# A vision layer on one core: the prologue of its attention part in another order, images 0 and 1 in buffers of their own

## The chip, the core and the metric

One core of a Trainium2 chip runs the whole program. The metric is the device time of one execution in microseconds (us); a kernel is given by the median of its runs. The engines are TensorE (PE, matmuls; PEld is its weight load), VectorE (DVE), ScalarE (ACT), GpSimd (POOL) and SyncE (SP, which here only starts transfers). They run side by side and wait for each other on semaphores that are written out by hand.

## What is computed

16 images of 5 x 128 x 128 are cut into 256 patches each of 320 numbers and embedded by a 320 x 256 matrix with a layernorm and `gamma`. Then comes one layer of 16-head attention whose scores are multiplied by a decay instead of a softmax, and one mixture of 8 experts:

```
h = layernorm(tokens @ W) * gamma
x = layernorm(h)
q, k = silu(x @ Wq), silu(x @ Wk);  v = x @ Wv
cum = cumsum(-softplus(x @ Wa + ba));  decay[i, j] = exp(cum[i] - cum[j]) for j <= i, else 0
o = groupnorm(((q @ k.T) * decay) @ v) * gn_w + gn_b
h = h + (o * sigmoid(x @ Wg)) @ Wo
h = h + top2_experts(layernorm(h))
```

## The kernel before

The attention part handles the images in eight pairs `p` of two images (512 columns), and each pair in eight steps `c` of two heads. `step(p, c)` exists once for every compute engine and lists, in a fixed order, what that engine does in this step: `scores`, `weighted`, `queries`, `keys`, `gates`, `values` on TensorE; `tanh_q`, `tanh_k`, `tanh_g`, `decay`, `keep_v`, `keep_o` on ScalarE; `silu_q`, `silu_k`, `decayed` on VectorE; `decay_rows` (the causal mask) on GpSimd. The same steps embed the images of the next pair, finish the attention of the pair before (groupnorm, `out_proj`) and route the rows of the pair before that. An engine never takes an instruction out of its order; a wait holds up all that stands behind it. The experts follow after the last pair and are not touched.

What matters here is the start, the steps of `p = -1`, in which only the work for pair 0 is done:

- An image's embedding: `load_patches(n)` (L351) brings 256 KB + 64 KB into `xt`; `tokens(n)` (L1105) makes 12 matmuls into bank 6; `embed(n)` (L1590) takes statistics and writes `h1`; `embed_rsqrt(n)` (L657) on GpSimd raises the variances to -1/2; `embed_norm(n)` (L1612) writes `xn1`; `turn(n)` (L1117) transposes it into bank 6; `keep_xnT(n)` (L747) copies that into `xs`; `scaled_h(n)` (L771) and `store_h(n)` send `h1` to DRAM. There is one `xt`, one bank, one `h1`, one `xn1` and one set of small statistics tiles for all images, so each image waits for the one before.
- The five weights `wv, wq, wk, wg, wo`, 1 MB each, come through three staging buffers in `big_f` (`load_weight`, L442). Each is split into a high part on ScalarE (`weight_hi`, L782) and a low part on VectorE (`weight_lo`, L1649), as every projection is made of three fp32r products. The pair's `xs` is split likewise (`xn_hi`, `xn_lo`).
- The decay: `logits(0)` (L1125), `decay_logits`, `softplus`, `log_decay`, `cum` (L1133), `running_sums`, `cum_rows`, `keep_cum` (L777); `store_cum(0)` writes the sums to DRAM and `load_decay` (L368) reads them back, spread over all partitions, in a ring of four; then `decay_rows`, `decay`, and `decayed`, which multiplies the scores.

All loads but some constants on GpSimd's queue are issued by SP, in this order: `wt`, patches 0, four constants, weight 0 (`wv`), patches 1, weights 1 and 2, `store_h(0)`, weight 3, patches 2, `store_h(1)`, weight 4, `store_cum(0)`, four decay loads. TensorE's own order of the start, by `step(-1, c)`: `tokens(0)`, `turn(0)`, `tokens(1)`, `turn(1)`, `logits`, `cum`, `cum_rows`, `tokens(2)`, `queries(0,0)`, `values(0,0)`, `keys(0,0)`, `values(0,1)`, `gates(0,0)`, and then `step(0, 0)` with `scores(0,0,0)`, `queries(0,1)`, `values(0,2)`, `values(0,3)`, `weighted(0,0,0)`. On ScalarE and VectorE the split of a weight stands at the head of a step:

```
            def start(c):
                if c == 0:
                    weight_hi(0)
...
            for c in range(NP):
                if c in (1, 3, 4, 6, 7):
                    weight_lo({1: 0, 3: 1, 4: 2, 6: 3, 7: 4}[c])
                step(-1, c)
```

Of the kernel before, what the change touches and what calls it, by code (L numbers as in the profile page):

```python
# [75 lines left out]
def vit_layer(nc, xT, w_tok, gamma, wq, wk, wv, wg, wa, ba, wo, gn_w, gn_b,  # L76
# [3 lines left out]
    with ExitStack() as ctx:  # L80
# [2141 lines left out]
```

## Time and profile before

| what | before |
|---|---|
| timed runs, us | 1323.49, 1326.96, 1327.07 |
| median, us | 1326.96 |
| the profiled execution: its time, us | 1323.79 |
| its span, us | 1321.9 |
| TensorE busy, us (share) | 1250.9 (95%) |
| ScalarE busy | 858.5 (65%) |
| VectorE busy | 825.2 (62%) |
| GpSimd busy | 428.1 (32%) |
| mean granted TensorE clock | 0.983 |

The span runs from the first to the last instruction. Busy time counts no waits. The granted clock is 1.00 at 2.4 GHz and 0.50 at 1.2 GHz. Matmuls are pipelined and their ends are modelled, so the busy time of TensorE says that it has work, not that it is at its peak. In the page's table of 40 slices (33 us each) the first slice shows TensorE 3 tenths busy, the second 8, every one of the others but the last 9 or more.

### The profile page before, as it was taken

The page shows a single profiled execution, that of the slowest core. Times are in us where ns is not written, and L with a number is a line of the kernel's source. Part 1 is how long each engine was busy: PE and PEld are TensorE (multiplying, and loading weights), DVE is VectorE, ACT ScalarE, POOL GpSimd, SP SyncE. Part 2 cuts the span into 40 slices and gives each one's busy share as a digit, 9 for nine tenths or more (in the row PEclk, how much of TensorE's full clock was granted, in tenths as well). Part 3 has the DMA queues.
Part 4 walks back from the last instruction along what each step waited for, and adds up shares of the span by engine and source line. Part 5 has one row for each costly group of instructions (what it writes and reads, how often), then busy time and mean ns, then how long its engine had stood idle before and what let it go on. Part 6 is the DMA issues. An engine that isn't in the chain of part 4 may idle for free. (4 is left out here: it accounts for less than half of the span.)

```text
span 1321.9 us, 27298 instructions
## 1 busy us (share of the span) xinstructions
PE 1250.9 (95%) x8534; PEld 1072.3 (81%) x8534; DVE 825.2 (62%) x2119; ACT 858.5 (65%) x2019; POOL 428.1 (32%) x524
## 2 busy tenths in 40 slices
PE   3899999999999999999999999999999999999996
PEld 2676777878778778778778778889999999989996
DVE  4455556665665665665665566657788888565552
ACT  2557577576576576576576565636788888666662
POOL 2021211241241241241141142164444544433434
PEclk7799999999999999999999999999999999999998
DMA  5321331341331331341332236458888787888873
GB/s 193 121 93 61 105 98 47 117 131 46 117 129 49 109 128 57 108 130 57 108 114 63 89 102 186 161 179 245 282 238 222 222 237 188 262 257 262 249 232 88
DMA packets 125607, 194.46 MB, mean 147 GB/s; under 512 B 16272, under 2 KB 91504, under 8 KB 125360
## 3 DMA queue, kind: packets, MB, share of 16 engines
q1 hardware_dynamic: 111920, 175.91, 41.5%
q0 software_dynamic: 13584, 17.26, 6.4%
q8 instruction: 54, 0.88, 0.3%
q14 instruction: 49, 0.40, 0.1%
HBM read 167.40 MB, written 29.05 MB: 149 GB/s over the span
## 5 line engine op out<-in xcount | busy, mean ns | idle before, releaser
L1161 PE MATMUL bank<-xn_sp,big_r 128*128 128x512 f32 x1152 | 312.1, 408 | 0.0
L1161 PEld LDWEIGHTS bank<-xn_sp,big_r 128*128 128x128 f32 x1152 | 204.6, 188 | 53.2 <-issue 1.4
L1674 DVE TENSOR_TENSOR att<-bank,dec_x 128x384 f32<-128x384 f32 x256 | 130.7, 552 | 110.1 <-PE bank L1198 108.9
L817 ACT ACTIVATE dec_x<-dec_x,ncum 128x256 f32<-128x256 f32 (+1 forms) x512 | 189.7, 444 | 5.7 <-POOL dec_x L654 5.7
L654 POOL TENSOR_SCALAR_AFFINE_SELECT dec_x<-dec_x 128x256 f32<-128x256 f32 x256 | 103.6, 434 | 215.8 <-DMA dec_x<-cum_scratch 215.7
L1494 PE MATMUL bank<-big_r 128*128 128x256 f32 x1296 | 168.0, 286 | 1.5 <-ACT mid_f L887 1.0
L1494 PEld LDWEIGHTS bank<-big_r 128*128 128x128 f32 x1296 | 160.5, 192 | 3.3 <-ACT mid_f L887 1.4
L705 POOL TENSOR_SCALAR mid_f<-mid_f,dec_x 128x256 f32<-128x256 f32 x71 | 76.9, 1087 | 187.0 <-DVE mid_f L1925 184.6
L711 POOL DMA_INDIRECT out<-mid_f,tok x71 | 118.6, 1671 | 53.0 <-POOL mid_f L705 22.0
L1941 DVE TENSOR_TENSOR big_r<-mid_f,big_r 128x256 fp32r<-128x256 f32 x216 | 91.4, 424 | 69.5 <-ACT big_r L907 69.3
L887 ACT ACTIVATE mid_f<-bank,h 128x256 f32<-128x256 f32 x216 | 101.2, 477 | 43.5 <-PE bank L1494 22.1
L789 ACT ACTIVATE tq<-bank 128x512 f32<-128x512 f32 x64 | 38.3, 598 | 140.3 <-PE bank L1161 140.3
L1932 DVE TENSOR_TENSOR big_r<-big_f,big_r 128x512 fp32r<-128x512 f32 x148 | 102.0, 695 | 7.1 <-ACT big_r L881 0.4
L1154 PE MATMUL bank<-big_r,xn_sp 128*128 128x512 f32 x384 | 97.7, 393 | 0.0
L1237 PEld LDWEIGHTS bank<-big_r,y_sp 128*128 128x128 f32 x768 | 95.5, 191 | 1.9
L1237 PE MATMUL bank<-big_r,y_sp 128*128 128x256 f32 x768 | 96.8, 284 | 0.0
L794 ACT ACTIVATE tq<-bank 128x512 f32<-128x512 f32 x64 | 38.2, 596 | 89.2 <-PE bank L1161 89.1
L1209 PE MATMUL bank<-att,mid_f 128*64 128x256 f32 x512 | 85.6, 407 | 10.4 <-ACT big_f L822 8.0
L1195 PE MATMUL bank<-q_s,k_s 64*128 64x256 f32 x512 | 91.0, 432 | 4.2 <-issue 4.2
L676 POOL DMA_INDIRECT expert_rows<-xn,slot x64 | 69.0, 1078 | 76.6 <-DVE slot L1809 60.4
L881 ACT ACTIVATE big_r<-big_f 128x512 fp32r<-128x512 f32 x148 | 93.5, 636 | 0.0
L907 ACT ACTIVATE big_r<-mid_f 128x256 fp32r<-128x256 f32 x216 | 91.7, 425 | 0.0
(217 smaller groups left out, 2231.4 us busy)
## 6 DMA issues: line engine op xcount, KB each, us to landing
big_f<-in_L_ffn_w SPq DMA_DIRECT2D x68, 1024.0 KB, 6.2
dec_x<-cum_scratch SPq DMA_DIRECT2D x128, 384.0 KB, 3.5
big_w<-in_L_ffn_w SPq DMA_DIRECT2D x12, 1024.0 KB, 6.7
mid_f<-expert_rows SPq DMA_DIRECT2D x27, 261.0 KB, 3.4
xt<-in_x SPq DMA_DIRECT2D x16, 256.0 KB, 3.7
h_scratch<-h SPq DMA_DIRECT2D x16, 256.0 KB, 2.3
h<-h_scratch SPq DMA_DIRECT2D x8, 512.0 KB, 4.3
out<-h SPq DMA_DIRECT2D x16, 256.0 KB, 4.0
```

The lines of the kernel that those rows point to most:

```text
L654: pool.affine_select(out=d, in_=d, pattern=[[0, 2], [1, P]], compare_op=ALU.is_ge, fill=fill, base=0, channel_multiplier=-1).then_inc(M["c ...
L711: pool.indirect_dma_start(out=out_rows, out_offset=bass.IndirectOffsetOnAxis(ap=tok[k.par][:, s:s + 1], axis=0), in_=yo[k.par][:, s, :], i ...
L817: act.activation(d, d, ACT.Exp, bias=ncum[p % 2][:, NS * u + s, 2 * c + hh:2 * c + hh + 1]).then_inc(M["exp_done"], 1)
L881: act.activation(parts[0].rearrange("p k n -> p (k n)")[:, cols], staged[:, cols], ACT.Copy).then_inc(M[f"{name}_hi"], 1)
L887: act.activation(target, bank[hbank[c % HB]][:, 0:width], ACT.Gelu_apprx_tanh, bias=b1_sb[k.par][:, c:c + 1]).then_inc(M["gel_done"], 1)
L907: act.activation(g_sp[0][:, c, :], gel[c % NGEL], ACT.Copy).then_inc(M["gh_done"], 1)
L1154: mm = pe.matmul(bank[target][:, :], xp[:, k, t * P:(t + 1) * P], wp[:, k, n * 512:(n + 1) * 512], start=(k == 0 and j == 0), stop=(k == E ...
L1161: mm = pe.matmul(bank[target][:, :], wp[:, k, c * P:(c + 1) * P], xp[:, k, :], start=(k == 0 and j == 0), stop=(k == EC - 1 and j == 2))
L1237: mm = pe.matmul(bank[target][:, s * E:(s + 1) * E], yp[:, j, u * S + s * P:u * S + (s + 1) * P], wp[:, GC * g + j, :], start=(j == 0 and ...
L1494: mm = pe.matmul(bank[hbank[c % HB]][:, 0:BLK], wp[:, i, c * P:(c + 1) * P], xp[:, i, :], start=(i == 0 and j == 0), stop=(i == EC - 1 and ...
L1674: dve.tensor_tensor(att[hh][:, :], bank[4 + hh][:, 0:LW], dec[n % RING][:, hh, :], ALU.mult).then_inc(M["mult_done"], 1)
L1932: dve.tensor_tensor(lo, staged[:, cols], f32(hi), ALU.subtract).then_inc(M[f"{name}_lo"], 1)
```

## The change

- Image 1 gets side buffers: patches, `h` and normed rows in parts of `mid_f` (where `v_sb` lies later), its small tiles in `pick`, which moves up; and bank 1. Image 2's tokens go to bank 7.
- Weights come in the order `wq, wv, wk, wg, wo`, with a staging buffer each for the first four; `wo` takes the second one again, after `ws_lo` 2.
- ScalarE issues the loads of `wt` and of the four constants, SP the rest in a new order.
- The loops over `step(-1, c)` give way to lists of functions on TensorE, ScalarE and VectorE. `values(0, 2)` and `values(0, 3)` and their copies are in the list, with banks 2 to 5 for the four, and no longer in `step(0, 0)`. The split of `wo` moves behind `step(0, 1)`.
- The waits follow: `tokens(0..2)` no longer wait for earlier images, `keep_v(0, 2)` and `keep_v(0, 3)` wait for image 1's side buffers, the first `scores` for the copies from banks 4 and 5.

```diff
-        stage_w = [big_f[:, i:i + 2048] for i in (0, 2048, 6144)]
+        stage_w = [big_f[:, i:i + 2048] for i in (0, 2048, 4096, 6144, 2048)]
...
+        side_x = [xt, mid_f[:, 2048:2048 + (KT + 1) * S].rearrange("p (k n) -> p k n", k=KT + 1)]
+        side_h = [h1, mid_f[:, 2816:3328].rearrange("p (s n) -> p s n", s=NS)]
+        side_n = [xn1, mid_f[:, 3328:3840].rearrange("p (s n) -> p s n", s=NS)]
+        little = pick[:, :, :, :].rearrange("p t k n -> p (t k n)")
+        side_st = [st1, little[:, 0:6].rearrange("p (s k) -> p s k", s=NS)]
+        side_su = [st1u, little[:, 6:12].rearrange("p (s k) -> p s k", s=NS)]
+        side_rs = [rs1, little[:, 12:16].rearrange("p (j s) -> p j s", j=2)]
+        side_ep = [eps0, little[:, 16:18]]
+        def of(n, buffers):
+            return buffers[1 if n == 1 else 0]
+        def embed_bank(n):
+            return {1: 1, 2: 7}.get(n, 6)
...
-        W_ATT = [wv, wq, wk, wg, wo]
-        w_parts = [wsp[2], wsp[0], wsp[1], wsp[3], wo_sp]
+        W_ATT = [wq, wv, wk, wg, wo]
+        W_IN = [("ws_in0", 1), ("ws_in1", 1), ("ws_in2", 1), ("ws_in3", 1), ("ws_in1", 2)]
+        w_parts = [wsp[0], wsp[2], wsp[1], wsp[3], wo_sp]
...
             def load_patches(n):
-                have(sp, "tok_ps", n)
-                image = xT[:, n * S:(n + 1) * S]
-                sp.dma_start(xt[:, 0:KT, :], image[0:KT * P, :].rearrange("(k p) n -> p k n", p=P)).then_inc(M["xt_in"], 16)
-                sp.dma_start(xt[0:KREM, KT, :], image[KT * P:FEAT, :]).then_inc(M["xt_in"], 16)
+                have(sp, "tok_ps", {1: 0, 2: 1}.get(n, n))
+                image, to, m = xT[:, n * S:(n + 1) * S], of(n, side_x), "xt_in1" if n == 1 else "xt_in"
+                sp.dma_start(to[:, 0:KT, :], image[0:KT * P, :].rearrange("(k p) n -> p k n", p=P)).then_inc(M[m], 16)
+                sp.dma_start(to[0:KREM, KT, :], image[KT * P:FEAT, :]).then_inc(M[m], 16)
...
+            def load_weight(i):
+                have(sp, "ws_lo", 2 if i == 4 else 0)
+                sp.dma_start(stage_w[i].rearrange("p (k n) -> p k n", k=EC if i < 4 else NP),
+                             W_ATT[i].rearrange("(k p) n -> p k n", p=P)).then_inc(M[W_IN[i][0]], 16)
             load_patches(0)
-            for dst, src in ((gammaB[:, :], gamma.rearrange("(a n) -> a n", a=1).broadcast_to([P, E])),
-                             (ident[:, :], ident_d),
-                             (baB[:, :], ba.rearrange("(a n) -> a n", a=1).broadcast_to([P, H])),
-                             (wa_sb[:, :, :], wa.rearrange("(k p) n -> p k n", p=P))):
-                sp.dma_start(dst, src).then_inc(M["c_in"], 16)
-            def load_weight(i):
-                have(sp, "ws_lo", i - 2)
-                sp.dma_start(stage_w[i % 3].rearrange("p (k n) -> p k n", k=EC if i < 4 else NP),
-                             W_ATT[i].rearrange("(k p) n -> p k n", p=P)).then_inc(M[f"ws_in{i % 3}"], 16)
+            load_patches(1)
             load_weight(0)
-            load_patches(1)
             load_weight(1)
+            load_patches(2)
             load_weight(2)
+            load_weight(3)
             store_h(0)
-            load_weight(3)
-            load_patches(2)
             store_h(1)
-            load_weight(4)
             store_cum(0)
             for c in range(2):
                 for u in range(2):
                     load_decay(0, c, u)
+            load_weight(4)
...
+            act.dma_start(wt[:, 0:KT, :], w_tok[0:KT * P, :].rearrange("(k p) n -> p k n", p=P)).then_inc(M["wt_in"], 16)
+            act.dma_start(wt[0:KREM, KT, :], w_tok[KT * P:FEAT, :]).then_inc(M["wt_in"], 16)
+            for dst, src in ((gammaB[:, :], gamma.rearrange("(a n) -> a n", a=1).broadcast_to([P, E])),
+                             (ident[:, :], ident_d),
+                             (baB[:, :], ba.rearrange("(a n) -> a n", a=1).broadcast_to([P, H])),
+                             (wa_sb[:, :, :], wa.rearrange("(k p) n -> p k n", p=P))):
+                act.dma_start(dst, src).then_inc(M["c_in"], 16)
...
+                if p == 0 and t >= NS and n == 0:
+                    act.wait_ge(M["tok_ps"], 2)
+                    act.wait_ge(M["h_out"], 32)
...
-            for c in range(NP):
-                start(c)
-                step(-1, c)
+            weight_hi(0)
+            weight_hi(1)
+            keep_xnT(0)
+            weight_hi(2)
+            keep_xnT(1)
+            xn_hi(0)
+            softplus(0)
+            scaled_h(0)
+            scaled_h(1)
+            tanh_q(0, 0)
+            keep_cum(0)
+            weight_hi(3)
+            for i in range(TP):
+                keep_v(0, i, 2 + i)
+            decay(0, 0, 0)
+            tanh_k(0, 0)
+            tanh_g(0, 0)
+            decay(0, 0, 1)
             for p in range(NPR):
                 for c in range(NP):
                     step(p, c)
+                    if p == 0 and c == 1:
+                        weight_hi(4)
 
...
+                if n == 1:
+                    pe.wait_ge(M["xt_in1"], 32)
+                else:
+                    pe.wait_ge(M["xt_in"], 32 * max(n, 1))
...
+                if n == 0:
+                    pe.wait_ge(M["v_done"], TP)
...
-                    if c == 0:
+                    if c == 0 and p > 0:
...
             tokens(0)
+            tokens(1)
             pe.wait_ge(M["c_in"], 64)
             pe.wait_ge(M["c_sum"], 32)
-            for c in range(NP):
-                step(-1, c)
+            turn(0)
+            tokens(2)
+            turn(1)
+            logits(0)
+            queries(0, 0)
+            values(0, 0, 2, "s1_xnT", 2)
+            values(0, 1, 3, "s1_xnT", 2)
+            cum(0)
+            values(0, 2, 4, "s1_xnT", 2)
+            cum_rows(0)
+            values(0, 3, 5, "s1_xnT", 2)
+            keys(0, 0)
+            gates(0, 0)
             pe.wait_ge(M["g_in"], 16 * 7)
...
-            for c in range(NP):
-                if c in (1, 3, 4, 6, 7):
-                    weight_lo({1: 0, 3: 1, 4: 2, 6: 3, 7: 4}[c])
-                step(-1, c)
+            embed(0)
+            embed_norm(0)
+            embed(1)
+            embed_norm(1)
+            weight_lo(0)
+            xn_lo(0)
+            decay_logits(0)
+            weight_lo(1)
+            log_decay(0)
+            weight_lo(2)
+            running_sums(0)
+            silu_q(0, 0)
+            weight_lo(3)
+            silu_k(0, 0)
             dve.wait_ge(M["g_in"], 16 * 7)
             dve.tensor_scalar(gnwh[:, :], gnw[:, :], 0.5, None, ALU.mult).then_inc(M["gnh"], 1)
             dve.tensor_scalar(gnbh[:, :], gnb[:, :], 0.5, None, ALU.mult).then_inc(M["gnh"], 1)
...
             for p in range(NPR):
                 for c in range(NP):
                     step(p, c)
+                    if p == 0 and c == 1:
+                        weight_lo(4)
```

In `embed`, `embed_norm`, `scaled_h`, `store_h`, `embed_rsqrt` and `turn` the tiles of image `n` are picked by `of(n, ...)`, and waits for the image before fall away for image 1.

## Rows read from the trace of the kernel before

**Rows 1.** Busy time by stretch: PE, PEld, DVE, ACT, POOL (x instructions), clock, DMA share, GB/s

```profile
6.30:40.00 33.70, 15.54 (x52) 12.53 (x52) 14.75 (x25) 13.37 (x15) 4.38 (x3) 0.65 0.58 192
57.00:350.00 293.00, 286.19 (x1825) 224.89 (x1824) 170.69 (x390) 186.08 (x415) 63.62 (x119) 1.00 0.28 91
```

**Rows 2.** Timeline of the prologue: start, us, engine, line, operation [idle before <- releaser]

```profile
1.84 0.56 SPq L354 DMA_DIRECT2D xt<-in_x  x1
...
6.33 4.46 PE L1113 MATMUL bank<-wt,xt 128*128 128x256 f32 x12 [6.33 <-DMA xt<-in_x]
...
10.90 0.70 DVE L1596 BATCH_NORM_STATS2 st<-bank 128x6 f32<-128x512 f32 x1 [9.39 <-PE bank L1113]
...
12.99 1.91 ACT L784 ACTIVATE big_r<-big_f 128x2048 fp32r<-128x2048 f32 x1 [11.00 <-DMA big_f<-in_L_attn_Wv]
...
13.67 1.05 POOL L660 TENSOR_TENSOR rs<-rs,mhalf 128x4 f32<-128x4 f32 x1 [7.03 <-DVE rs L1609]
...
14.93 2.29 DVE L1651 TENSOR_TENSOR big_r<-big_f,big_r 128x2048 fp32r<-128x2048 f32 x1 [1.35 <-ACT big_r L784]
...
18.02 1.08 PE L1122 MATMUL bank<-ident,turned 128*128 128x128 f32 x4 [7.24 <-DVE turned L1617]
...
19.88 4.51 PE L1113 MATMUL bank<-wt,xt 128*128 128x256 f32 x12 [0.78 <-ACT xs L753]
...
27.19 2.99 POOL L660 TENSOR_TENSOR rs<-rs,mhalf 128x4 f32<-128x4 f32 x1 [12.47 <-DVE rs L1609]
...
32.88 3.59 PE L1129 MATMUL bank<-wa_sb,xs 128*128 128x16 f32 x16 [0.69 <-ACT xs L753]
...
42.12 0.27 ACT L780 ACTIVATE cumT<-bank 64x128 f32<-64x128 f32 x1 [1.44 <-PE bank L1145]
```

**Rows 3.** Timeline from the cumulative sums to the first steps of the loop

```profile
42.54 5.12 PE L1113 MATMUL bank<-wt,xt 128*128 128x256 f32 x12 [0.45 <-ACT cumT L780]
...
50.93 1.48 ACT L817 ACTIVATE dec_x<-dec_x,ncum 128x256 f32<-128x256 f32 x4
...
52.32 0.58 ACT L794 ACTIVATE tq<-bank 128x512 f32<-128x512 f32 x1
...
52.93 0.69 DVE L1665 SCALAR_TENSOR_TENSOR k_s<-tq,bank 128x512 f32<-128x512 f32 x1 [2.54 <-ACT tq L794]
...
54.41 0.70 PE L1195 MATMUL bank<-q_s,k_s 64*128 64x256 f32 x4
...
56.76 2.90 PE L1154 MATMUL bank<-big_r,xn_sp 128*128 128x512 f32 x12
```

**Rows 4.** Busy time by stretch: the loads at the start

```profile
2.00:10.00 8.00, 3.67 (x10) 3.03 (x11) 0.00 (x0) 0.00 (x0) 4.64 (x9) 1.00 0.91 263
10.00:12.00 2.00, 0.78 (x4) 0.35 (x2) 1.07 (x2) 0.00 (x0) 0.00 (x0) 1.00 0.16 58
14.00:19.00 5.00, 0.98 (x4) 0.71 (x4) 2.94 (x3) 0.90 (x1) 0.72 (x1) 0.50 0.99 368
```

**Rows 5.** Timeline further on, at full clock: step (0,2), and the logits of pair 1

```profile
77.18 1.02 DVE L1674 TENSOR_TENSOR att<-bank,dec_x 128x384 f32<-128x384 f32 x2 [3.62 <-PE bank L1198]
...
78.49 2.75 PE L1113 MATMUL bank<-wt,xt 128*128 128x256 f32 x12
...
78.69 0.60 ACT L789 ACTIVATE tq<-bank 128x512 f32<-128x512 f32 x1 [1.74 <-PE bank L1161]
...
104.21 1.85 PE L1129 MATMUL bank<-wa_sb,xs 128*128 128x16 f32 x16
```

**Rows 6.** Busy time by stretch: where the granted clock changes

```profile
22.00:24.00 2.00, 2.00 (x7) 1.64 (x7) 0.00 (x0) 2.00 (x2) 0.00 (x0) 0.68 0.93 283
26.00:28.00 2.00, 0.00 (x0) 0.00 (x0) 1.93 (x6) 0.00 (x0) 0.81 (x1) 0.68 0.35 120
46.00:48.00 2.00, 2.00 (x8) 1.61 (x7) 0.00 (x0) 0.00 (x0) 0.00 (x0) 0.71 0.28 112
```

More of the change, by code:

```diff
@@ L946, in step @@
                     decay(p, c + 1, 0)
-                    for i, source in {0: ((2, 2), (3, 1)), 1: ((4, 2),), 3: ((7, 2),)}.get(c, ()):
+                    for i, source in {0: ((2, 2), (3, 1)) if p > 0 else (), 1: ((4, 2),), 3: ((7, 2),)}.get(c, ()):
                         keep_v(p, i, source)
@@ L980, in step @@
                     tanh_g(p, c + 1)
-            def start(c):
-                if c == 0:
-                    weight_hi(0)
-                if c == 2:
-                    weight_hi(1)
-                if c == 3:
-                    weight_hi(2)
-                if c == 5:
-                    weight_hi(3)
-                if c == 6:
-                    weight_hi(4)
-            for c in range(NP):
-                start(c)
-                step(-1, c)
+            weight_hi(0)
[16 more added lines that the diff above has]
+            decay(0, 0, 1)
             for p in range(NPR):
@@ L1112, in tokens @@
                     for k in range(KT + 1):
-                        mm = pe.matmul(bank[6][:, s * E:(s + 1) * E], xt[:, k, s * P:(s + 1) * P], wt[:, k, :],
+                        mm = pe.matmul(bank[embed_bank(n)][:, s * E:(s + 1) * E], of(n, side_x)[:, k, s * P:(s + 1) * P], wt[:, k, :],
                                        start=(s == 0 and k == 0), stop=(k == KT), skip_group_check=True)
@@ L1121, in turn @@
                     for s in range(NS):
-                        mm = pe.transpose(bank[6][:, k * S + s * P:k * S + (s + 1) * P], xn1[:, s, k * P:(k + 1) * P], ident[:, :])
+                        mm = pe.transpose(bank[1 if n == 1 else 6][:, k * S + s * P:k * S + (s + 1) * P], of(n, side_n)[:, s, k * P:(k + 1) * P], ident[:, :])
                 mm.then_inc(M["s1_tps"], 1)
@@ L1149, in values @@
                 t, n = i % TP, i // TP
+                if p == 0 and i == 0:
+                    pe.wait_ge(M["ws_lo"], 2)
                 pe.wait_ge(M["xl_done"], p + 1)
@@ L1593, in embed @@
                 dve.wait_ge(M["tok_ps"], n + 1)
-                have(dve, "h_out", 16 * n)
-                rows = bank[6][:, :].rearrange("p (s n) -> p s n", s=NS)
+                have(dve, "h_out", 16 * n if n > 1 else 0)
+                h1, st1, st1u, rs1, eps0 = (of(n, x) for x in (side_h, side_st, side_su, side_rs, side_ep))
+                rows = bank[embed_bank(n)][:, :].rearrange("p (s n) -> p s n", s=NS)
                 dve.bn_stats(st1[:, :, :].rearrange("p s k -> p (s k)"), rows.rearrange("p s n -> p n s")).then_inc(M["s1_st"], 1)
@@ L1600, in embed @@
                                              op0=ALU.subtract, op1=ALU.mult).then_inc(M["s1_u"], 1)
-                have(dve, "s1_h", NS * n)
+                have(dve, "s1_h", NS * n if n > 1 else 0)
                 dve.tensor_scalar(rs1[:, 0, :], st1[:, :, 2], 1.0 / E, EPS, ALU.mult, ALU.add).then_inc(M["s1_v0"], 1)
@@ L1613, in embed_norm @@
                 dve.wait_ge(M["s1_rs"], n + 1)
-                have(dve, "s1_tps", n)
+                have(dve, "s1_tps", n if n > 1 else 0)
                 have(dve, "lg_ps", 2 * (n // 2 - 2))
+                h1, xn1, st1u, rs1 = (of(n, x) for x in (side_h, side_n, side_su, side_rs))
                 for s in range(NS):
```

37 lines of the change are left out of this document (16 added, 21 removed).

## The prediction, made before the change was run

> **What bounds the kernel now.** I read the table of stretches first [rows 1]. From 57 to 350 us TensorE is busy for 286.2 of 293 us at a granted clock of 1.00; from 6.3 to 40 us it stands still more than it works (15.5 busy of 33.7 us). So the main loop is bound by TensorE, and what happens before the first `scores` is a serial prologue whose length goes straight into the time. The timeline of the prologue [rows 2] says what it waits for. Image 0: `tokens(0)` 6.33 to 10.79, its statistics, then 2.29 us of `weight_lo(0)` ahead of `embed_norm(0)`, so `turn(0)` starts only at 18.02. Image 1 can't start before image 0 has left `xt`, bank 6 and `h1`: `tokens(1)` at 19.88, and so on. Here GpSimd's power took 2.99 us beside a `weight_lo`, against 1.05 for image 0. Then `logits` at 32.88, `cum`, `cum_rows`, `keep_cum` at 42.12. From there a fixed chain leads to the loop [rows 3]: `keep_cum` at 42.12, the decay rows through DRAM (first exponential 50.93), `tanh_k` and `silu_k`. The first `scores`, at 54.41, comes right behind `gates`, so at that point the decay chain and TensorE end nearly together.
>
> The profiled execution took 1323.79 us for a span of 1321.9. Of the three timed runs one (1323.49) lies with it and two (1326.96, 1327.07) lie 3 us higher, the median among them. I sum against 1323.8 and correct at the end.
>
> **The change, part by part.**
>
> *Loads.* Six issues, some 0.56 us each, leave SP's queue for ScalarE's; two of them stood ahead of the patches of image 0 (issued at 1.84, rows 2), which now go out 1.1 us earlier. ScalarE pays the same issues in time in which it waits for the first weight (11.00 us idle before 12.99, rows 2), so they cost nothing; without that cover, 3 us. The 16 DMA engines are already 0.91 busy from 2 to 10 us [rows 4]. If bytes decide and three queues now share them, `tokens(0)` gains nothing or loses 0.5; if the issue decides it gains 1.1. I take 0.5: 5.8 to 10.3. The Trainium skill (DMA: Bandwidth & Descriptors, section "Issuing engines are not separate DMA queues") says that loads started on several engines run on the same 16 DMA engines and that only the issuing time is saved; by that the gain here would be near nothing, 6.3 instead of 5.8. Whichever bound `tokens(0)` takes, the end of the chain doesn't move, as the next part shows.
>
> *Bytes ahead of image 2.* In the new order SP issues patches 0, patches 1, Wq, Wv, and then, after `tokens(0)`, patches 2, Wk, Wg. TensorE's new order is `tokens(0)`, `tokens(1)`, `turn(0)`, `tokens(2)`, `turn(1)`: image 1's turn stands behind image 2's load. Up to the end of patches 2 that is 320+216 KB on ScalarE's queue, 292 KB on GpSimd's and 3 x 320 + 2 x 1024 on SP's: 3836 KB, 3.93 MB. By 10 us the old trace had moved 8 us x 263 GB/s = 2.10 MB; then SP's queue ran dry (58 GB/s to 12 us), which it no longer does. The other 1.83 MB at the 368 GB/s of Wq and Wk together (14 to 19 us) take 5.0 us, to 15.0; Wv's semaphore came some 2 us behind its bytes (the rate fell away at 10, it was used at 12.99), so patches 2 are there at about 16.8. Bound: 16.0 with one us of tail, 19.0 at the 263 GB/s of the first 10 us.
>
> *Images 0 and 1.* `tokens(1)` follows at once, 2.75 us at full clock [rows 5], 4.5 at half: 13.1 to 14.8. VectorE: `embed(0)` 10.4 to 13.2 (10.90 to 13.67, where GpSimd's power begins, before), power 1.05, norm 0.73: 15.0; `embed(1)` the same, 19.7. No `weight_lo` stands between. All of it is hidden under the load of patches 2. `tokens(2)` takes 4.5 at low clock, 16.8 to 21.3, `turn(1)` 0.7 to 22.1, `keep_xnT(1)` 0.6 to 22.7. ScalarE must have done `weight_hi(2)` by then: Wk lands 1.05/0.368 = 2.9 us behind patches 2, at 19.7, plus 1.91 [rows 2] is 21.6. Just in time; if it is late, `keep_xnT(1)` is queued behind it.
>
> *Logits to cumulative rows.* `logits` took 3.59 us at half clock [rows 2], 1.85 at full [rows 5]; I take 3.0: 25.9. `xn_hi`, `xn_lo` (1.04, 1.22) fit in, to 25.1. `zb`, `zm` to 26.4; `weight_lo(1)`, 2.28, to 28.7 with softplus (0.26 x 3 and a 1.28 table load) under it; `la` 28.9. `queries`, six matmuls like a `values`, is hidden under `weight_lo(1)`; `values` 0 and 1 wait for it. At 1.45 us each at full clock (two of them took 2.90, rows 3) and up to twice that at half, I take 4.1 for the two: 32.8. `cum` 0.8, 33.6; `running_sums` 0.5 while `values(2)` runs to 35.1; `cum_rows` 0.4, `keep_cum` 0.3: 35.85, against 42.39 before. The bounds are 34.5 (all at full clock) and 38.5 (all at half).
>
> *The fixed chain.* Store, decay loads and mask until the first exponential took 50.93 - 42.39 = 8.54 us. ScalarE now runs `weight_hi(3)` and four `keep_v` (1.9 + 4 x 0.6 = 4.3) under it and `decay(0,0,0)` ahead of `tanh_k`: 1.48 + 0.58 + 0.69 + gaps 0.1. Together 11.4: first `scores` at 47.3, 7.1 earlier. `weight_lo(3)` (37.8 to 40.0) and `gates` (to 41.6) are under it too, and TensorE idles from 41.6 to 47.3.
>
> *Work moved out of the loop.* `values` 2 and 3, 2.90 us on a TensorE that is busy without a gap [rows 1, 3], now lie in the prologue: gain 2.9. Their copies overwrite image 1's side buffers, so they wait for `h_out`: `scaled_h(1)` ends about 31, store 2.3 later, long before 37.8.
>
> *What is given back.* (a) Clock. The granted clock fell from 1.00 (2.4 GHz) to 0.50 (1.2 GHz) at 26.7, 2.3 us after `tokens(1)` had ended, and went up at 23.3, when TensorE had worked 3.4 us from 19.88, and at 47.2, 4.6 us from 42.54 [rows 2, 3, 6]; the moments are worked out from the mean clock of the 2 us stretches. After 5.7 idle us I count it low at 47.3: about 4 us of work at half speed, 2.0 lost. Bounds 0 and 2.3. (b) Wo's split. `weight_hi(4)` (1.91) and `weight_lo(4)` (2.29) move into the end of step (0,1). ScalarE waited 1.74 there and VectorE 3.62 [rows 5]; the split delays `decayed(0,2,0)` by some 3.5 us, of which `tokens(3)` covers all but about 1. I take 1.0, bounds 0 and 3. Wo's load, 1 MB behind the first four decay loads, is over by 49 and next asked for 15 us later; nothing.
>
> Sum: 7.1 + 2.9 - 2.0 - 1.0 = **7.0 us**, 1316.8 for an execution like the profiled one. The runs shown spread from there to 3 us above; I put the median in between, at 1317.5.
>
> **The rivals.**
>
> *Loads decide (0.2).* ScalarE's order puts `weight_hi(1)` and `weight_hi(2)` ahead of `keep_xnT`. If the loads keep the first 10 us' 263 GB/s instead of 368, Wk comes at (2.88 MB / 0.26) 21.1 plus 2 = 23.1, its split ends at 25.0, `keep_xnT(1)` at 25.6, 2.9 later than above: gain 4.1, 1319.7. For it: three queues with many small packets share the engines. Against: Wq and Wk, loaded together, ran at 368 [rows 4].
>
> *The clock stays up (0.2).* Prologue and loop start lose nothing to it: `keep_cum` 1.3 earlier, 2.0 not lost, Wo's split covered: 7.0 + 4 = 11, 1313. Against: the fall in rows 6 came after 2.3 idle us, against 5.7 here.
>
> *The gain is swallowed later (0.1).* Some later stage waits for a transfer or a scatter and starts when it did before: 1323.8. Against: from 57 to 350 us TensorE is 98% busy [rows 1], and nothing in it goes by absolute time.
>
> *Slower (0.04).* The clock, once low at the first `scores`, stays low because the loop's first steps now wait for decay and Wo's split between short bursts. Every us of TensorE work at half speed costs one; against 10.0 - 1.0 gained, it decides from 9 us of work (done in 18) on, and at 14 the time is 1329. Against: through the same steps the old trace reads 1.00 to 350 us [rows 1].
>
> *My forecast, 0.46.* A measurement of this kernel can tell some 0.3% (4 us) from no change. Half of "loads decide" lies at that edge. Faster: 0.46 + 0.2 and most of the 0.2, 0.82; same 0.14; slower 0.04. The range takes in 1313 and its run spread less one, and on the other side the swallowed gain: 1311.5 to 1323.5.
>
> **What would show it.** In the trace after: `tokens(1)` right behind `tokens(0)`; `tokens(2)` waiting for patches 2 until near 16.8 and `turn(1)` near 21.5; `keep_cum` near 35.6; first `scores` near 47.3 with an idle TensorE and a clock of 0.50 before it; from 100 us on all instructions 7 us earlier. It is wrong if `keep_xnT(1)` is released by `weight_hi(2)`, if the clock in the stretch behind the first `scores` is 1.00, or if TensorE has gaps of several us around Wo's split.

## The result and the profile after

| what | before | after |
|---|---|---|
| runs, us | 1326.96, 1323.49, 1327.07, 1321.96, 1323.44 | 1316.64, 1312.47, 1314.73, 1314.97, 1319.66 |
| median, us | 1323.49 | 1314.97 |
| profiled execution, us | 1323.79 | 1316.64 |
| its span, us | 1321.9 | 1314.6 |
| TensorE busy, us | 1250.9 | 1251.5 |
| mean granted clock | 0.983 | 0.986 |

The ratio after to before is 0.9936, 95% interval 0.9917 to 0.9955: faster by 0.6%, 8.5 us by the medians, and "no change" (a ratio of 1) lies outside the interval. The kernel before has five runs here instead of three, and its median is 1323.49 instead of 1326.96.

TensorE has the same work in the same time; what is gone is idle time at the start. The stretches of the kernel after, with the columns of [rows 1]:

```profile
6.30:40.00 33.70, 26.50 (x101) 21.18 (x101) 16.98 (x29) 16.70 (x21) 2.40 (x3) 0.85 0.46 162
57.00:350.00 293.00, 286.17 (x1826) 225.24 (x1825) 175.18 (x411) 187.35 (x415) 64.04 (x119) 1.00 0.28 90
```

Against [rows 1], TensorE works 26.5 instead of 15.5 us before 40, and the main loop is the same to 0.02 us. The timeline of the prologue after, which answers to [rows 2] and [rows 3]:

```profile
7.25 4.94 PE L1140 MATMUL bank<-wt,xt 128*128 128x256 f32 x12 [7.25 <-DMA wt<-in_L_tok_W]
...
12.02 2.75 PE L1140 MATMUL bank<-wt,mid_f 128*128 128x256 f32 x12
...
14.54 0.70 DVE L1638 BATCH_NORM_STATS2 st<-bank 128x6 f32<-128x512 f32 x1 [12.77 <-DMA wa_sb<-in_L_attn_Wa]
...
19.29 1.09 PE L1149 MATMUL bank<-ident,turned 128*128 128x128 f32 x4 [4.51 <-DVE turned L1660]
...
20.16 5.22 PE L1140 MATMUL bank<-wt,xt 128*128 128x256 f32 x12
...
25.23 0.60 PE L1149 MATMUL bank<-ident,mid_f 128*128 128x128 f32 x4
...
26.51 1.96 PE L1156 MATMUL bank<-wa_sb,xs 128*128 128x16 f32 x16 [0.69 <-ACT xs L770]
...
31.65 3.07 PE L1183 MATMUL bank<-big_r,xn_sp 128*128 128x512 f32 x12
...
36.70 0.27 ACT L797 ACTIVATE cumT<-bank 64x128 f32<-64x128 f32 x1 [2.10 <-PE bank L1172]
...
45.34 1.49 ACT L837 ACTIVATE dec_x<-dec_x,ncum 128x256 f32<-128x256 f32 x4 [4.65 <-POOL dec_x L663]
...
48.29 1.23 PE L1226 MATMUL bank<-q_s,k_s 64*128 64x256 f32 x4 [5.48 <-DVE k_s L1708]
```

`tokens(1)` follows `tokens(0)` at full clock. But the first statistics wait until 14.54 for the last of the four constants, though `tokens(0)` ended at 12.2, and `tokens(2)` starts right behind `turn(0)`, not when patches 2 come. The list of transfers gives the time from the start of an issue to landing (last number, us):

```profile
gammaB<-in_L_tok_gamma ACTq DMA_DIRECT2D x1, 128.0 KB, 5.8
ident<-in_c_ident ACTq DMA_DIRECT2D x1, 64.0 KB, 6.5
baB<-in_L_attn_ba ACTq DMA_DIRECT2D x1, 8.0 KB, 8.2
wa_sb<-in_L_attn_Wa ACTq DMA_DIRECT2D x1, 16.0 KB, 10.8
```

They were issued at 1.85, 2.70, 3.20 and 3.71, so they landed at 7.7, 9.2, 11.4 and 14.5. The statistics read none of them; `embed(0)` needs only `gammaB`, which was there before `tokens(0)` ended, and `wa_sb` is first read by `logits`, at 26.51. VectorE waits ahead of `embed(0)` because the program has one wait for all four there (`c_in` at 64, 16 for each), as TensorE has ahead of `turn(0)`. From `keep_cum` at 36.70 the decay chain leads to the first `scores` at 48.29, 6.1 earlier than in [rows 3], behind 5.48 idle us of TensorE.

The start of the last `tokens` matmul of the attention part is a mark that the noise of the whole time does not reach. This is the row of the `tokens` matmuls, of before and then of after (duration min/median/max, first and last start):

```profile
L1113 PE MATMUL bank<-wt,xt x192: 377/379/767, 6.3 to 675.7; 128*128 128x256 f32 x192
```

```profile
L1140 PE MATMUL bank<-wt,xt x180: 377/379/794, 7.2 to 669.1; 128*128 128x256 f32 x180
```

675.7 - 669.1 = 6.6 us is what the prologue brings. What follows that mark took 646.2 us before and 645.5 after; over all fourteen profiles of this study it took 643.8 to 649.2, while the changed kernel, profiled twice, has the mark at 669.1 and 668.6. So the prologue is read from this mark, and whole times need several runs.

### The profile page after: what moved, and what is told of

Its sections match the earlier page's. It is cut to its first block and busy times, and to the rows that moved or that the text cites. A ratio compares the mean times of both kernels' runs of the same rounds, so it can differ in the third digit from the quotient of the medians.

```text
span 1314.6 us, 27299 instructions
## 1 busy us (share of the span) xinstructions
PE 1251.5 (95%) x8534; PEld 1072.4 (82%) x8534; DVE 824.6 (63%) x2120; ACT 858.2 (65%) x2019; POOL 425.4 (32%) x524
## 5 line engine op out<-in xcount | busy, mean ns | idle before, releaser
L837 ACT ACTIVATE dec_x<-dec_x,ncum 128x256 f32<-128x256 f32 (+1 forms) x512 | 189.7, 444 | 10.4 <-POOL dec_x L663 10.4
L1240 PE MATMUL bank<-att,mid_f 128*64 128x256 f32 x512 | 86.4, 407 | 10.5 <-ACT big_f L842 8.0
```

The source lines that it names most:

```text
L837: act.activation(d, d, ACT.Exp, bias=ncum[p % 2][:, NS * u + s, 2 * c + hh:2 * c + hh + 1]).then_inc(M["exp_done"], 1)
```

## The experiments

Every kernel below is the changed one with the edit shown. All start times in us; "scores" and "weighted" are the first ones of the loop, "mark" is the mark above, "time" that of the profiled execution, the only one for the kernels from consts_sp to wo_early. A time holds the scatter behind the mark, so these kernels are compared by their marks: values_back, for one, is 7.2 us slower than the changed kernel by its time and 3.4 by its mark.

| kernel | tokens(0) | statistics | turn(1) | keep_cum | scores | weighted | mark | time |
|---|---|---|---|---|---|---|---|---|
| before | 6.33 | 10.90 | 31.10 | 42.12 | 54.41 | 59.59 | 675.7 | 1323.79 |
| after | 7.25 | 14.54 | 25.23 | 36.70 | 48.29 | 52.63 | 669.1 | 1316.64 |
| consts_sp | 6.16 | 11.03 | 20.66 | 33.59 | 45.51 | 49.95 | 667.1 | 1317.06 |
| all_sp | 6.25 | 11.82 | 21.03 | 33.18 | 44.95 | 49.39 | 666.0 | 1314.48 |
| act_order | 13.15 | 17.50 | 26.99 | 38.20 | 49.90 | 54.00 | 670.6 | 1320.99 |
| tok1_late | 5.75 | 14.95 | 30.23 | 43.13 | 55.20 | 59.42 | 675.9 | 1321.83 |
| values_back | 5.68 | 15.27 | 25.62 | 37.70 | 49.31 | 55.96 | 672.5 | 1323.80 |
| tok2_late | 6.49 | 15.94 | 25.14 | 39.18 | 50.39 | 52.83 | 669.6 | 1317.04 |
| warm | 5.85 | 15.53 | 24.87 | 36.07 | 47.74 | 52.18 | 669.6 | 1319.64 |
| cum_first | 5.67 | 14.68 | 24.13 | 31.88 | 44.30 | 48.74 | 666.1 | 1312.23 |
| wo_early | 5.91 | 15.83 | 26.20 | 39.11 | 50.85 | 55.29 | 672.2 | 1319.51 |
| best_a | 6.27 | 11.27 | 21.70 | 29.45 | 42.01 | 46.45 | 663.7 | 1311.31 |
| best_b | 6.46 | 11.65 | 20.86 | 29.22 | 41.82 | 44.26 | 660.9 | 1307.33 |
| again | 6.54 | 15.77 | 25.38 | 36.57 | 48.05 | 52.08 | 668.6 | 1314.77 |

The low clock at the first `scores` lasts longer in some of these profiles than in others. From the first to the second `weighted` it takes 4.6 to 4.7 us in nine of them, but 5.1 to 5.5 in consts_sp, warm, cum_first, wo_early and best_a, where the clock came back only behind the first `weighted`. So these five are 0.4 to 0.9 us worse at the mark than their first `weighted` says. From the second `weighted` to the mark the changed kernel and those made from it all take 611.9 to 612.2 us (wo_early 611.7, before 611.5).

**Where the loads are issued: consts_sp, all_sp, act_order.**

consts_sp puts the loop over the four constants back on SP:

```diff
             load_patches(0)
+            for dst, src in ((gammaB[:, :], gamma.rearrange("(a n) -> a n", a=1).broadcast_to([P, E])),
...
+                sp.dma_start(dst, src).then_inc(M["c_in"], 16)
             load_patches(1)
...
-                act.dma_start(dst, src).then_inc(M["c_in"], 16)
```

> The four constants (gammaB, ident, baB, wa) go back to SP's queue, behind patches 0; all else as in the changed kernel. Theory A (constants decide): in the changed kernel VectorE's first statistics waited until 14.54 for the last constant, 2.2 us after tokens(0) had ended; from there a chain norm, turn(0), tokens(2), turn(1) runs without slack. So here the statistics start with the end of tokens(0) near 12.3, turn(0) near 17.1 instead of 19.3, tokens(2) near 18, turn(1) near 23 instead of 25.2, keep_cum near 34.7 instead of 36.7, first scores near 46.3 instead of 48.3. Rival B (patches 2 decide, my forecast): tokens(2) starts when patches 2 land and stays within 0.5 us of 20.2, whatever the statistics do.

all_sp is consts_sp and

```diff
+            sp.dma_start(wt[:, 0:KT, :], w_tok[0:KT * P, :].rearrange("(k p) n -> p k n", p=P)).then_inc(M["wt_in"], 16)
+            sp.dma_start(wt[0:KREM, KT, :], w_tok[KT * P:FEAT, :]).then_inc(M["wt_in"], 16)
             load_patches(0)
...
-            act.dma_start(wt[:, 0:KT, :], w_tok[0:KT * P, :].rearrange("(k p) n -> p k n", p=P)).then_inc(M["wt_in"], 16)
-            act.dma_start(wt[0:KREM, KT, :], w_tok[KT * P:FEAT, :]).then_inc(M["wt_in"], 16)
```

> All six loads go back to SP's queue in the old order (wt, patches 0, constants), then patches 1, Wq, Wv and so on as in the changed kernel. Theory A (sharing between queues costs, the issue time does not matter): tokens(0) starts near 6.3 as in the kernel before, instead of 7.25, the statistics near 10.9, turn(0) near 15.7, first scores 3 us earlier than in the changed kernel, if patches 2 are there by 16.8. Rival (issuing on ScalarE helps): tokens(0) starts later than 7.25 and the first scores stay at 48.3 or move later by the 3 us of issues.

In consts_sp the statistics start at the end of `tokens(0)`:

```profile
11.03 0.70 DVE L1638 BATCH_NORM_STATS2 st<-bank 128x6 f32<-128x512 f32 x1 [9.26 <-PE bank L1140]
```

Theory A held, by more than it said for `turn(1)`: 4.6 earlier, not 2.2 (1.1 of it from `tokens(0)`). Of that 3.1 reached `keep_cum`, as `values` 0 and 1 ran at low clock here (4.54 us against 3.07), and 2.0 the mark. Patches 2 had landed by 16.27, where `tokens(2)` starts without a wait. In all_sp `tokens(0)` starts at 6.25, the mark is 3.1 earlier, and now `tokens(2)` does wait for patches 2:

```profile
17.74 2.86 PE L1140 MATMUL bank<-wt,xt 128*128 128x256 f32 x12 [0.55 <-DMA xt<-in_x]
```

So issuing on ScalarE made the prologue longer by 3.1 us at the mark (by 2.4 in best_a against cum_first, below). Whether it is the small transfers themselves that are slow on ScalarE's queue, the next kernel asks, with the order on that queue turned round:

```diff
-            act.dma_start(wt[:, 0:KT, :], w_tok[0:KT * P, :].rearrange("(k p) n -> p k n", p=P)).then_inc(M["wt_in"], 16)
-            act.dma_start(wt[0:KREM, KT, :], w_tok[KT * P:FEAT, :]).then_inc(M["wt_in"], 16)
...
                 act.dma_start(dst, src).then_inc(M["c_in"], 16)
+            act.dma_start(wt[:, 0:KT, :], w_tok[0:KT * P, :].rearrange("(k p) n -> p k n", p=P)).then_inc(M["wt_in"], 16)
+            act.dma_start(wt[0:KREM, KT, :], w_tok[KT * P:FEAT, :]).then_inc(M["wt_in"], 16)
```

> ScalarE issues the four constants first and wt behind them; nothing else differs from the changed kernel. In the runs with the constants last on ScalarE's queue their last semaphore came at 14.5 to 15.9 us, with them on SP's ahead of the large weights the statistics started right behind tokens(0) at 11.0 and 11.8. Theory A (the small loads share the DMA engines with Wq and Wv from the moment those are issued at 3.0 us, and what is behind wt falls into that): the constants, 1.1 us earlier and ahead of wt, are there before tokens(0) ends, the statistics start within 0.3 us of the end of tokens(0), at the price of wt, so tokens(0) starts 0.5 to 2 us later than 7.25; first scores 0 to 2 us earlier than 48.29. Rival B (loads from ScalarE's queue of such small rows are slow in themselves): the statistics still wait for a constant until after 13.5, and start later than the end of tokens(0).

```profile
13.15 4.25 PE L1140 MATMUL bank<-wt,xt 128*128 128x256 f32 x12 [13.15 <-DMA wt<-in_L_tok_W]
...
17.50 0.70 DVE L1638 BATCH_NORM_STATS2 st<-bank 128x6 f32<-128x512 f32 x1 [15.72 <-PE bank L1140]
```

The constants are no longer waited for: the last of them, issued at 2.21, landed 5.8 us later, at 8.0, against 7.7 to 8.2 where they go out on SP's queue ahead of the weights (consts_sp, all_sp, best_a, best_b). So rival B, small rows being slow on ScalarE's queue in themselves, is out. Now `wt` comes at 13.15, 5.9 us later, which neither theory had (A said 0.5 to 2), and the first `scores` are 1.6 later, not 0 to 2 earlier. What stands last in ScalarE's queue lands at 13 to 16, as Wq and Wv do, which were issued on SP's queue from 3.0 on (used at 12.9 and 15.2 in act_order). In these 10 us the queue of `wt` brought little: its 320 KB landed at 10.2 and 13.1, when the 1 MB of Wq, issued between its two parts, was there at 12.9. Sharing with the large loads fits all of these landing times; the bytes of each queue over time were not measured, so it stays an explanation that is argued. The Trainium skill (DMA: Bandwidth & Descriptors, section "Queues, rings and completion order") says that each DMA engine takes turns between its queues packet by packet. My inference from that, which it does not state: a queue with rows of 64 B to 1 KB moves fewer bytes in a turn than one with the weights' 4 KB rows. The landing times don't speak against it. The rule of the Trainium skill that the prediction weighed (DMA: Bandwidth & Descriptors, section "Issuing engines are not separate DMA queues"), that only the issuing time is saved, gives no reason for this cost. What was saved for `tokens(0)` is small and not steady: it starts at 5.7 to 7.3 over the eight profiles with `wt` first and the constants behind it, and at 6.2 to 6.5 with all on SP.

**The overlap of images 0 and 1: tok1_late.**

```diff
             tokens(0)
-            tokens(1)
...
             turn(0)
+            tokens(1)
             tokens(2)
             turn(1)
```

> tokens(1) goes behind turn(0) again; image 1 keeps its buffers. Theory A (overlap of the images gives the gain): embed(1) then starts only when tokens(1) ends, near 23.5 to 24.5, norm(1) near 28, turn(1) near 28.5 instead of 25.2, first scores 3 us later than 48.29. Rival B (the order of TensorE hides it, as turn(1) stands behind tokens(2) anyway): turn(1) moves by less than 1 us.

Theory A, and twice its size: the mark is at 675.9, so the whole gain is gone, and the first `scores` come 6.9 later instead of 3. `turn(1)` comes 5.0 later. Another 1.4 go to `logits`, in this row against 1.96 us in the kernel after:

```profile
31.55 3.40 PE L1156 MATMUL bank<-wa_sb,xs 128*128 128x16 f32 x16 [0.69 <-ACT xs L770]
```

TensorE had nothing from 28.1 to 30.2 here, and the granted clock was 0.50 from 31.8 to 38.6. In the kernel after `turn(1)` and `logits` follow `tokens(2)` closely at 1.00. `tokens(1)` itself took 4.94 us here, at low clock, against 2.75 right behind `tokens(0)`. So the order costs by the chain and by the clock that it brings, and this kernel does not separate the two.

**The work moved out of the loop: values_back.**

```diff
-            values(0, 2, 4, "s1_xnT", 2)
-            values(0, 3, 5, "s1_xnT", 2)
...
-                    if c == 0 and p > 0:
+                    if c == 0:
```

> values(0,2) and values(0,3) and their copies go back from the prologue to step (0,0). Theory A: in the changed kernel they run under the decay chain, so the prologue does not get shorter: keep_cum some 1.5 us earlier at best, as values(0,2) stands ahead of cum_rows, but the loop carries 2.9 us more; weighted(0,0,0) at 52.6 plus 1.5 to 2.9, and the span 1.5 to 2.9 us longer. Rival B (no worth in it): the prologue gets shorter by what the loop gets longer, weighted(0,0,0) stays within 0.5 us of 52.63.

The mark is 3.4 later. The statistics came 0.7 late, as the constants landed later than in the kernel after (14.5 to 15.9 over the eight profiles with that order), and `values` 0 and 1 ran at a low clock (below); `scores` is 1.0 later. From `scores` to `weighted` it takes 6.65 instead of 4.34 us, 2.3 more. The two add up to the 3.4. Theory A, for the 2.3: these matmuls are free under the decay chain, and in the loop they are paid.

**The clock at the first scores: tok2_late and warm.**

tok2_late:

```diff
             turn(0)
-            tokens(2)
             turn(1)
...
             gates(0, 0)
+            tokens(2)
```

> tokens(2) goes from between turn(0) and turn(1) to behind gates(0,0), into the 5.5 us in which TensorE idles before the first scores. Theory A (position): turn(1) starts when norm(1) is done, near 23.6 instead of 25.2; the gap before the first scores is filled, so the granted clock stays 1.00 there and scores and queries(0,1) take 3.0 us in place of 4.7. Against it: without tokens(2) the clock is 0.50 through logits (3.6 instead of 2.0 us) and the first values (2.6 instead of 1.5 each), so keep_cum gains nothing or comes up to 2 us later. Sum: weighted(0,0,0) between 1 us earlier and 1.5 us later than 52.63. Rival B (the clock follows neither): keep_cum 1.6 earlier and weighted 1.6 or more earlier.

warm, with matmuls of data that is there anyway:

```diff
             gates(0, 0)
+            pe.wait_ge(M["ct_copied"], 1)
+            for i in range(14):
+                pe.matmul(bank[6][:, :], wsp[0][0][:, 0, 0:P], xn_sp[0][:, 0, :], start=True, stop=True)
```

> 14 matmuls of 512 columns whose result nobody reads stand between gates(0,0) and the first scores, with all else as in the changed kernel: the cost of the clock by itself. Theory A (the idle 5.5 us drop the clock and cost the loop's start): with them the clock is 1.00 from 48 us on, scores and queries(0,1) take 3.0 us in place of 4.7, weighted(0,0,0) comes 1.7 to 2.0 us earlier than 52.63. Rival B: weighted(0,0,0) waits for decayed(0,0,0) or for a copy and not for the clock, and moves by less than 0.5 us.

In tok2_late `weighted` follows `scores` by 2.44 us instead of 4.34: the low clock there costs 1.9 us (1.6 in `again`, where it took 4.03). Both halves of theory A showed: `logits` took 3.59, and `keep_cum` came 2.5 later (1.4 of it by constants that landed at 15.94). The mark is 0.5 later; with the constants as in the kernel after I estimate it 0.9 earlier (0.5 less the 1.4). The stretches around the first `scores`, in the kernel after, in tok2_late and in warm:

```profile
44.00:46.00 2.00, 0.00 (x0) 0.00 (x0) 0.00 (x0) 0.66 (x2) 0.80 (x3) 0.91 0.89 283
46.00:48.00 2.00, 0.00 (x0) 0.00 (x0) 0.66 (x2) 2.00 (x6) 0.74 (x2) 0.50 0.96 300
...
52.00:54.00 2.00, 2.00 (x16) 1.09 (x17) 0.63 (x1) 1.26 (x4) 0.00 (x0) 0.89 0.59 222
```

```profile
46.00:48.00 2.00, 1.89 (x9) 1.33 (x7) 0.00 (x0) 0.56 (x2) 0.78 (x2) 1.00 0.84 252
48.00:50.00 2.00, 0.00 (x0) 0.00 (x0) 0.56 (x1) 2.00 (x6) 1.10 (x3) 1.00 1.04 269
50.00:52.00 2.00, 1.61 (x11) 1.44 (x12) 1.11 (x5) 1.28 (x4) 0.47 (x3) 1.00 0.90 274
```

```profile
46.00:48.00 2.00, 0.26 (x2) 0.29 (x4) 0.84 (x3) 2.00 (x6) 0.32 (x1) 0.83 1.00 279
48.00:50.00 2.00, 2.00 (x10) 1.56 (x10) 0.50 (x2) 0.63 (x2) 0.90 (x3) 0.50 0.88 291
```

warm missed what it was made for. The added matmuls ended at 45.35, TensorE idled for 2.4 us, and the clock fell all the same at 47.3, 0.4 us ahead of the first `scores`; `scores` to `weighted` took 4.44 us. In tok2_late TensorE idled for 2.5 us (47.9 to 50.4) and the clock stayed up. So filling part of the gap did not make the clock safe, and warm shows nothing on the price of the clock: `weighted` is 0.45 earlier, but so are `keep_cum` and `scores` (0.6 and 0.55).

**The order ahead of the decay chain: cum_first.**

In the lists of TensorE, of VectorE and of ScalarE:

```diff
             queries(0, 0)
+            cum(0)
+            cum_rows(0)
             values(0, 0, 2, "s1_xnT", 2)
...
+            running_sums(0)
             weight_lo(2)
-            running_sums(0)
...
+            keep_cum(0)
             tanh_q(0, 0)
-            keep_cum(0)
```

> cum and cum_rows go ahead of all values, running_sums ahead of weight_lo(2), keep_cum ahead of tanh_q. Theory A (the decay chain through DRAM sets the first scores, 11.6 us behind keep_cum): keep_cum near 33.2 instead of 36.7, first mask near 41, first scores near 44.8 instead of 48.3, 3.3 us gained in the span. Rival B (TensorE or the splits decide): gates(0,0) and silu_k end at the same time as before and the first scores gain less than 1 us.

```profile
30.46 0.43 PE L1164 MATMUL bank<-la,upper 128*128 128x64 f32 x2 [0.98 <-DVE la L1675]
...
31.88 0.27 ACT L797 ACTIVATE cumT<-bank 64x128 f32<-64x128 f32 x1 [0.29 <-PE bank L1172]
...
44.30 1.23 PE L1226 MATMUL bank<-q_s,k_s 64*128 64x256 f32 x4 [4.24 <-DVE k_s L1708]
```

Theory A: `keep_cum` is 4.8 earlier (1.1 of it by an earlier `turn(1)`), `scores` 4.0, the mark 3.0. The changed kernel has its cumulative sums waiting behind three `values` (two ahead of `cum`, one ahead of `cum_rows`) and a `weight_lo` while the one chain with nothing to spare hangs on them. From `keep_cum` to `scores` it now takes 12.4 us instead of 11.6: the six issues that store the sums take 3.48 us instead of 2.65, for a reason that no run here looked for.

**Wo's split: wo_early.**

```diff
+            load_weight(4)
             store_cum(0)
...
                 keep_v(0, i, 2 + i)
+            weight_hi(4)
...
-                    if p == 0 and c == 1:
-                        weight_hi(4)
...
             weight_lo(3)
+            weight_lo(4)
             silu_k(0, 0)
...
-                    if p == 0 and c == 1:
-                        weight_lo(4)
```

> Wo is loaded before the decay rows and split in the prologue, while ScalarE and VectorE wait for the first mask, and no longer behind step (0,1). Theory A (the split in the loop costs 0.4, as weighted(0,2,0) shows against the kernel before: 6.59 earlier behind it, 6.99 ahead of it): 0.4 us less from 75 us on, first scores unchanged at 48.3. Rival B (the prologue has no room): Wo's load delays cum's store or the split delays tanh_k, first scores later by 1 us or more.

From `weighted(0,0,1)` to `weighted(0,2,1)` the loop takes 22.91 us (60.48 to 83.39) against 23.32 (57.24 to 80.56) in the kernel after, so the split in the loop costs 0.4 us, as theory A has it. Its other half, `scores` unchanged, failed. The first `scores` came 2.56 later: 1.0 of it had come by the log decay (`la` at 32.26 instead of 31.28, behind later constants), and 1.4 came because `values` 0 and 1 took 4.51 us instead of 3.07. That is not the split but the clock, which stayed low until 36 instead of 32 us. So rival B's number came (1 us or more later), but not by its reason: from `keep_cum` to `scores` it took 11.7 us against 11.6. The mark is 3.1 later. The stretches of the kernel after and of wo_early:

```profile
30.00:32.00 2.00, 2.00 (x6) 1.50 (x5) 2.00 (x3) 1.99 (x5) 0.00 (x0) 0.51 0.00 0
32.00:34.00 2.00, 2.00 (x10) 1.62 (x9) 1.71 (x1) 1.97 (x4) 0.00 (x0) 1.00 0.56 215
```

```profile
32.00:34.00 2.00, 2.00 (x6) 1.42 (x6) 2.00 (x3) 1.98 (x6) 0.00 (x0) 0.50 0.12 49
34.00:36.00 2.00, 2.00 (x6) 1.56 (x5) 0.68 (x1) 1.56 (x2) 0.00 (x0) 0.50 0.85 269
```

**Put together: best_a and best_b, beside the changed kernel again.** best_a is all_sp with cum_first. best_b adds tok2_late and fills the old place of `tokens(2)`:

```diff
             turn(0)
+            for s in range(NS):
+                for k in range(KT + 1):
+                    pe.matmul(bank[7][:, s * E:(s + 1) * E], side_x[1][:, k, s * P:(s + 1) * P], wt[:, k, :],
+                              start=(s == 0 and k == 0), stop=(k == KT), skip_group_check=True)
             turn(1)
```

> All loads on SP as in all_sp, and cum first as in cum_first. If the two gains lie one behind the other on the same chain (theory A): all_sp starts the last tokens 3.1 us earlier than the changed kernel and cum_first 3.0, so here they start 6 us earlier, at 663, first scores near 41.3, and the time is 0.5% under the changed kernel's, near 1309. Rival B (weight_lo or the loads of Wk and Wg now decide): less than 4.5 us, last tokens at 664.6 or later.

> As best_a, with tokens(2) behind gates(0,0), and twelve matmuls of image 1's patches into the empty bank 7, whose result nobody reads, in its old place between turn(0) and turn(1). Theory A (the clock at the first scores costs 1.9 us, as tok2_late showed: 2.44 us from scores to weighted in place of 4.34, and the early clock hangs on work in that place, logits 3.38 without it and 1.96 with it): last tokens 1.5 to 2 us earlier than in best_a, logits 2.0 us. Rival B (the clock falls anyway behind tokens(2), as it fell behind the idle matmuls of warm after 2 us): 4.3 us from scores to weighted, within 0.5 us of best_a.

> The changed kernel once more, beside best_a and best_b on the same chip. Theory A: stages behind the prologue repeat to 0.1 us until 700 us, and the last tokens start at 669.1 give or take 1 us, by when the constants land; the spread of the whole time comes from the end, behind 700 us. Rival B: the main loop varies too, by more than 1 us between 100 and 700 us.

| kernel | runs | median, us | range, us | ratio to before (95%) |
|---|---|---|---|---|
| before | 17 | 1326.12 | 1321.44 to 1330.97 | |
| again (the changed kernel) | 12 | 1315.41 | 1313.04 to 1325.36 | 0.9930 (0.9911 to 0.9949) |
| best_a | 6 | 1311.29 | 1308.98 to 1313.49 | 0.9892 (0.9871 to 0.9913) |
| best_b | 5 | 1309.22 | 1307.33 to 1312.20 | 0.9883 (0.9860 to 0.9906) |

`again` bears out its theory A: the mark is at 668.6, within 1 us of 669.1; TensorE is busy for 243.97 us from 100 to 350 us against 243.94; and twelve runs of one kernel spread over 12 us.

best_a's mark is at 663.7, 5.4 before the changed kernel's: all_sp's 3.1 and cum_first's 3.0 lie behind each other, but for 0.7. (Against `again` it is 4.9.) best_b's is 2.8 earlier again; its rows:

```profile
16.86 2.76 PE L1455 MATMUL bank<-wt,mid_f 128*128 128x256 f32 x12
...
22.53 1.96 PE L1156 MATMUL bank<-wa_sb,xs 128*128 128x16 f32 x16 [1.05 <-ACT xs L770]
...
37.27 2.75 PE L1140 MATMUL bank<-wt,xt 128*128 128x256 f32 x12
...
41.82 0.70 PE L1226 MATMUL bank<-q_s,k_s 64*128 64x256 f32 x4 [1.80 <-DVE k_s L1712]
```

`logits` keeps its 1.96 us, `tokens(2)` fills the gap, and only 1.8 idle us are left before `scores`, which run at full clock: 2.44 us to `weighted`. That is all theory A asked for, and more than its 2 us, as best_a's low clock also cost 0.7 us behind the first `weighted` (5.31 us to the second, 4.62 in best_b). The theory's text has 3.38 us for `logits` without work in that place; the full row of tok2_late has 3.59. best_b is 6.2 us under the changed kernel by the medians; its interval and that of the changed kernel don't meet, while best_a's meets both. The marks order the three.

## Why the prediction was right, and where its steps were not

The forecast was 1317.5, in a range from 1311.5 to 1323.5; 7.0 us for an execution like the profiled one. The profiled ones differ by 7.15, the marks by 6.6, the medians by 8.5. The mechanism was right: a serial prologue, shortened by the overlap of the images and by work moved under the decay chain. That the sum came so near is in part luck. The terms as measured add up to 6.1 + 2.7 - 1.9 - 0.4 = 6.5, with misses of both signs, and the remaining 0.6 to the 7.15 lie behind the mark. Its terms:

- **Chain to the first scores, 7.1.** 6.1 came. *Patches 2 as the start of the chain* was the step that failed: "all of it is hidden under the load of patches 2" has the statistics at 10.4; they came at 14.54, as the four constants, moved to ScalarE's queue, landed late. I had counted their issue (nothing, rightly) and asked of the sharing only what it does to `tokens(0)`, not to what stands last in that queue. `turn(0)` was then 4.2 late against 15.1, and `tokens(2)` started at 20.16 instead of 16.8. The load itself had been sized well: `tokens(2)` waited for it until 17.74 in all_sp, and it was there by 16.27 in consts_sp. The wait of VectorE for all four constants ahead of `embed(0)` stood in the kernel before too; with the constants ahead of the weights it cost nothing there. The prediction never asked when the last of them would come.
- *Logits to cumulative rows*, 22.7 to the end of `keep_cum` at 35.85, was forecast as 13.1 us and took 10.5 (26.5 to 36.97), since the clock was up for more of it than I took: `logits` 1.96 instead of 3.0, `values` 0 and 1 3.07 instead of 4.1. This paid back 2.7 of the 3.8 us by which `logits` came late; two misses of opposite sign, and by luck: in `again`, the same kernel, the constants came 1.2 later still, the clock stayed up from `logits` on, and `keep_cum` came at 36.57.
- *The fixed chain* from the end of `keep_cum` to `scores`: 11.4 forecast, 11.3 measured (36.97 to 48.29).
- **Values moved, 2.9.** 4.34 us from `scores` to `weighted` instead of 5.18, with 1.9 more spent on the low clock, makes 2.7; values_back loses 2.3 there.
- **Clock, 2.0.** 1.9, by tok2_late (in other profiles up to 0.9 more, by when it came back); the fall at 45.6 and the rise at 52.4 stand in the stretches above. The rival "the clock stays up" is out for the changed kernel.
- **Wo's split, 1.0.** 0.4. From `weighted(0,0,1)` to `weighted(0,2,1)` it took 23.32 us against 22.92 before (64.23 to 87.15). The rows of the kernel after:

```profile
69.35 1.92 ACT L801 ACTIVATE big_r<-big_f 128x2048 fp32r<-128x2048 f32 x1
...
71.31 2.29 DVE L1694 TENSOR_TENSOR big_r<-big_f,big_r 128x2048 fp32r<-128x2048 f32 x1 [4.74 <-ACT big_r L801]
...
73.52 1.02 DVE L1717 TENSOR_TENSOR att<-bank,dec_x 128x384 f32<-128x384 f32 x2
```

`decayed` starts at 73.52, 3.3 later than [rows 5] less the 7.0 us by then (70.2), close to the 3.5 forecast; `tokens(3)` covers more of it than I took.

- **Loads decide.** Not by the mechanism named: `weight_hi(2)` was done at 22.8, ahead of `turn(1)`. But its argument for ("three queues with many small packets share the engines") points at what probably made the constants late.
- **Swallowed later** and **slower**: out. The loop is the same to 0.02 us; what follows the mark scatters by 5.4 us, with no sign of being longer after the change (645.5 and 644.1 us in the two profiles, 646.2 before).

## What to carry to other kernels

Spreading loads over two queues gives up their order: here small loads that were needed first had to stand on the same queue as the large ones, ahead of them. A wait for each constant only where it is first read might do as well, since `gammaB` had landed at 7.7; that was not run. In a prologue, follow the one chain that goes through DRAM and put everything else behind it. Idle time under such a chain is a free place for work of the loop. If that work reaches near the end of the gap it may save the clock as well: it did with 1.8 (best_b) and 2.5 idle us left (tok2_late), it did not with 2.4 (warm).

## What was not expected of the hardware

- The last of the constants (16 KB), issued by 4.2 us on ScalarE's queue behind `wt`, landed at 14.5 to 15.9 in the eight profiles with that order, beside 2 MB on SP's queue. Ahead of these on SP's it landed at 7.7 to 8.2.
- The clock fell 2.0 us into the 2.4 idle us of warm and stayed up over 2.5 in tok2_late. In the kernel after it also fell once with only 0.48 idle us in two, in the stretch in which `logits` ended. These are two stretches of the kernel after, and the second one in `again`, where with the same matmuls it stayed up:

```profile
26.00:28.00 2.00, 1.49 (x14) 1.49 (x14) 0.42 (x1) 1.51 (x2) 0.00 (x0) 1.00 0.00 0
28.00:30.00 2.00, 1.52 (x8) 1.26 (x8) 1.97 (x4) 0.98 (x3) 0.00 (x0) 0.64 0.00 0
```

```profile
28.00:30.00 2.00, 1.52 (x10) 1.32 (x10) 1.97 (x4) 0.82 (x3) 0.00 (x0) 1.00 0.00 0
```

- With the same matmuls in the same place, `values` 0 and 1 took 3.0 us in some kernels (warm, act_order, again) and 4.5 in others (wo_early, values_back, consts_sp), by when the clock came back. A prologue of this kind varies by 1.5 us for that alone.
- GpSimd's power took 1.02 to 1.05 us for images 0 and 1 in the kernel after, where no `weight_lo` runs beside it, against 2.99 for image 1 in [rows 2].
